# Queries and keys of an attention pair prepared three steps ahead of their scores instead of two

## The chip, the cores and the metric

The kernel runs on one core of a Trainium2 chip. A core has a matmul engine (PE), three engines for elementwise work (DVE, ACT, POOL) and a queue engine (SP) that issues transfers; each takes its own instructions in order, and they wait for each other on semaphores. The metric is device time in microseconds; lower is better.

## The reference

The input is a batch of 4 images of 32 x 32 tokens with 128 channels. The first layer is a shifted-window transformer block; the second is a self-attention over all 1024 tokens of an image. The change touches the window attention of the first layer alone. Cut to that:

```python
xn = _layer_norm(x, norm1_g, norm1_b)
xs = jnp.roll(xn, (-4, -4), axis=(1, 2))
xw = xs.reshape(B, nH, 8, nW, 8, 128).transpose(0, 1, 3, 2, 4, 5).reshape(64, 64, 128)
qkv = xw @ qkv_w.T + qkv_b                     # 16 heads of 8 channels
q = _rope2d(q); k = _rope2d(k)                 # rotation by the place in the window
attn = jnp.einsum('bhnd,bhmd->bhnm', q * scale, k) + attn_mask
attn = softmax(attn, axis=-1)
out = jnp.einsum('bhnm,bhmd->bhnd', attn, v)
```

Then come the output projection, a residual, a second layer norm, a gated MLP, and the second layer.

## The kernel before, in words

Two windows of 64 tokens make a pair of 128 rows; there are 32 pairs. The first half of the program, up to about 190 us, works them off in steps. All five engines run the same `body(n, it, w)`, each with its own part, from step `FIRST` on; steps 0 to 11 and the last ones are written out, steps 12 to 27 are two turns of a loop of eight. Several pairs are in flight. In step n, with the lines of the profile:

- PE projects queries and keys of pair n+2 (L899, L901), turns the rows of pair n+1 (L937, four matmuls for queries and four for keys), computes the scores of pair n (mask through L909, products L918), the transposed scores of pair n-1 (L909, L930), the values of pair n-3 (L991), the value projection of pair n-1 (L899, L901), and turns the query rows of pair n once more, now with the maxima in them (L937).
- DVE rotates pair n+2 (`ta`, `tb`, L1082), copies the turned rows of pair n+1 to `qk_t` (L1094), takes the low part of the values (L1102), the row maxima of pair n (L1109) and their two halves (L1114, L1116), and normalises pair n-3 (L1127, L1131).
- POOL adds `rot` (L1287), then takes the low part of the probabilities (`p_lo`, L1295), then the low parts of the query and key rows (L1299 to L1301).
- ACT makes the high parts of the rows (`q_rows`, `k_rows`, by the helper at L1151), the exponentials (L1221), the copy `q_t` of the second turning, the high values and `p_hi` (all L1151).
- SP waits for the copy `qk_t` and issues four transfers (L869) that spread the turned keys over `k_t`, in zeros. The scores of the pair wait for all four.

The four transfers of pair n+1 are issued in step n and their wait on PE is at the scores of step n+1:

```python
pe.wait_ge(kz_ready[u], it * 64 + 64)
wait(pe, mlo_done, n)
scores(qk_t[:, u, 0], k_t[:, r], w, parts).then_inc(s_done, 1)
```

The tiles `ta`, `tb`, `rot`, `k_rows` and `qk_t` have two buffers, `q_rows` and `k_t` four.

Beside the steps runs the first layer norm, in eight chunks of four pairs: statistics on DVE (L1026, L1030), the reciprocal root on POOL (L1264 to L1269), the normalisation on ACT (`xn`, L1165), the turning on PE (L878), and `xn_all` on ACT and DVE (L1151, L1045). Chunks 2 to 7 are turned in steps 1, 3, ... 11. In the negative steps POOL also clears half of `k_t` (L1305). In the last steps the first pieces of the MLP are interleaved (`mlp_early`).

## Time and profile before

| | us |
|---|---|
| median of 3 runs | 404.51 (403.96 to 408.64) |
| the profiled execution, its own time | 403.14 |
| its span in the trace | 401.3 |
| PE busy | 349.9 (87%) |
| DVE busy | 301.4 (75%) |
| ACT busy | 271.5 (68%) |
| POOL busy | 270.8 (67%) |

PE is the busiest engine of the whole span, but its busy time counts pipelined matmuls in full. The stages have to be read one by one: the ramp up to about 37 us, the steps with layer norm chunks up to about 88 us, the steps without them up to about 176 us, the last steps with the first MLP work up to about 195 us, and then the MLP and the second layer, in which the change has no instruction.

### The profile page before, as it was taken

The numbers are of one execution on the slowest core, as the hardware profiler recorded it, in microseconds if no ns is written. First come the engines' busy times: TensorE is split into PE (matmuls) and PEld (weight loads), VectorE is DVE, ScalarE is ACT, GpSimd is POOL, SyncE is SP. The second block draws the span as 40 slices with busy tenths as digits, with TensorE's granted clock in tenths as the row PEclk, the third lists the DMA queues.
The fourth block names the chain that finished last, engine by engine and source line by source line (L and its number), as shares of the span: only waits on it lengthen the run. The fifth ranks groups of instructions, "written<-read, shape, count | busy, mean of one in ns | idle before, by whom it ended". The sixth has DMA issues, their size and how long they took to land.

```text
span 401.3 us, 12541 instructions
## 1 busy us (share of the span) xinstructions
PE 349.9 (87%) x4900; PEld 228.5 (57%) x4900; DVE 301.4 (75%) x830; ACT 271.5 (68%) x435; POOL 270.8 (67%) x322
## 2 busy tenths in 40 slices
PE   2668999998989999998779899999988989989592
PEld 0335666555555666666456456654565757667371
DVE  6758988888878888888757678787668797883424
ACT  2466888887868788886835644445478877868480
POOL 7477976666767777798586786755267775867340
PEclk9999999999999999999999999999999999999797
DMA  6701111001111000010000000000000011010102
GB/s 187 244 19 28 29 28 26 23 24 31 28 29 30 26 26 26 26 33 11 2 3 2 15 13 2 2 2 2 9 19 22 7 54 28 2 54 2 52 2 57
DMA packets 15597, 12.29 MB, mean 31 GB/s; under 512 B 3992, under 2 KB 14137, under 8 KB 15545
## 3 DMA queue, kind: packets, MB, share of 16 engines
q1 hardware_dynamic: 14208, 11.03, 9.5%
q8 instruction: 36, 0.59, 0.7%
q10 hardware_dynamic: 1336, 0.54, 0.5%
q14 instruction: 17, 0.13, 0.1%
HBM read 4.22 MB, written 2.10 MB: 16 GB/s over the span
## 4 chain that ended last, share of the span: by engine, by line
PE 63%; DVE 16%; ACT 7%; issue 5%; DMA 4%; POOL 3%; SPq 1%; DVEq 0%; ACTq 0%; POOLq 0%
PE ps L359 8%; PE ps L1577 7%; PE ps L909 6%; PE ps L937 5%; PE ps L991 5%; PE ps L930 4%; PE ps L918 3%; PE ps L899 3%; DMA k_t<-qk_t 3%; PE ps L377 3%; PE ps L901 2%; DVE ob L1701 2%; DVE mx L1670 2%; PE ps L1417 2%; PE ps L373 2%
## 5 line engine op out<-in xcount | busy, mean ns | idle before, releaser
L1752 POOL TENSOR_TENSOR el<-e,eh 128x1024 f16<-128x1024 f32 x28 | 59.6, 2130 | 31.7 <-ACT eh L1744 31.4
L1295 POOL TENSOR_TENSOR p_lo<-e_buf,p_hi 128x1024 f16<-128x1024 f32 x32 | 68.2, 2130 | 4.8 <-ACT p_hi L1151 2.8
L359 PE MATMUL ps<-y_t,fc_w 128*128 128x512 f16 x192 | 46.2, 380 | 5.2 <-POOL al L273 2.5
L1287 POOL TENSOR_TENSOR rot<-ta,tb 128x256 f32<-128x256 f32 x32 | 23.3, 728 | 39.6 <-DVE tb L1082 38.8
L1109 DVE TENSOR_REDUCE ps<-ps 128x16 f32<-128x1024 f32 x32 | 39.4, 1232 | 8.3 <-PE ps L918 7.5
L1735 ACT ACTIVATE e<-ps 128x1024 f32<-128x1024 f32 x32 | 32.6, 1020 | 19.1 <-PE ps L1566 18.7
L1577 PE MATMUL ps<-val,eh 128*128 128x129 f16 x512 | 38.4, 225 | 7.8 <-DVE ob L1701 7.2
L909 PE MATMUL ps<-mask,identb 128*128 128x512 bf16 x128 | 39.4, 390 | 6.6 <-DMA k_t<-qk_t 6.5
L1221 ACT ACTIVATE e_buf<-ps 128x1024 f32<-128x1024 f32 x32 | 32.7, 1023 | 15.3 <-PE ps L930 15.1
L1577 PEld LDWEIGHTS ps<-val,eh 128*128 128x128 f16 x512 | 32.3, 100 | 18.6 <-issue 11.0
L288 POOL TENSOR_TENSOR hl<-hid,hh 128x512 f16<-128x512 f32 x24 | 27.7, 1158 | 20.4 <-DVE yn L566 11.2
L677 ACT ACTIVATE sg<-ps,fc_bias 128x512 f32<-128x512 f32 x32 | 21.9, 685 | 23.2 <-PE ps L359 23.0
L1670 DVE TENSOR_REDUCE mx<-ps 128x1 f32<-128x1024 f32 x24 | 29.3, 1223 | 8.8 <-PE ps L1550 8.4
L1151 ACT ACTIVATE p_hi<-e_buf 128x1024 f16<-128x1024 f32 x32 | 33.8, 1057 | 0.8
L1744 ACT ACTIVATE eh<-e 128x1024 f16<-128x1024 f32 x32 | 33.7, 1054 | 0.7
L359 PEld LDWEIGHTS ps<-y_t,fc_w 128*128 128x128 f16 x192 | 17.0, 98 | 27.9 <-issue 6.1
L937 PE MATMUL ps<-ident,q_rows 128*128 128x128 f16 x256 | 26.3, 227 | 6.5 <-DVE q_rows L1116 3.6
L529 DVE SCALAR_TENSOR_TENSOR hid<-ps,fc_bias,sg 128x512 f32<-128x512 f32 x32 | 23.8, 746 | 10.2 <-ACT sg L677 5.4
L899 PE MATMUL ps<-qkv_w,xn_all 128*128 128x128 f16 (+1 forms) x192 | 27.7, 254 | 2.5 <-DVE xn_all L1045 1.8
L930 PEld LDWEIGHTS ps<-q_t,k_t 128*64 128x64 f16 x1024 | 18.7, 112 | 13.6 <-issue 13.6
L1151 ACT ACTIVATE q_t<-ps 128x512 f16<-128x512 f16 x32 | 19.1, 596 | 10.4 <-PE ps L937 10.1
L1577 PE MATMUL ps<-val,el 128*128 128x129 f16 x256 | 23.8, 226 | 0.0
(164 smaller groups left out, 985.0 us busy)
## 6 DMA issues: line engine op xcount, KB each, us to landing
k_t<-qk_t SPq DMA_DIRECT2D x126, 32.0 KB, 1.9
x_all<-in_x SPq DMA_DIRECT2D x8, 256.0 KB, 4.4
out<-ob SPq DMA_DIRECT2D x8, 192.0 KB, 2.1
yr<-xr SPq DMA_DIRECT2D x16, 64.0 KB, 2.0
mask_f<-in_mask SPq DMA_DIRECT2D x1, 512.0 KB, 3.5
fc_w<-in_fc_w SPq DMA_DIRECT2D x1, 512.0 KB, 5.5
out<-ob SPq DMA_DIRECT2D x4, 128.0 KB, 1.9
fc_w<-in_fc_w SPq DMA_DIRECT2D x1, 256.0 KB, 5.4
```

The source lines that it names most:

```text
L359: last = pe.matmul(ps[:, bank, :], fc1_w16[:, ws, 128 * block_:128 * block_ + 128], y_t[:, v, ys, :], start=(n == 0), stop=(n == 2))
L899: pe.matmul(out, xn_all[:, at(i, 1), xs, :].rearrange("p a q -> p (a q)"), qkv_w16[:, ws, cols], start=(n == 0), stop=False, skip_group_ch ...
L909: pe.matmul(ps[:, bank + b, :].rearrange("p (h k) -> p h k", h=8), identb[:], mm, start=(part == 0), stop=False, skip_group_check=True)
L930: last = pe.matmul(ps[rows, ST_BANK + h // 8, WTOK * (h % 8):WTOK * (h % 8) + WTOK], keys[:, h % 4, h // 4, rows], queries[:, h // 4, rows ...
L937: last = pe.transpose(out[:, c, :], rows[:, 4 * c:4 * c + 4, :].rearrange("p h r -> p (h r)"), ident16[:])
L1109: dve.tensor_reduce(mx_ps, ps[:, S_BANK:S_BANK + 2, :].rearrange("p b (h k) -> p (b h) k", h=8), AX.X, ALU.max).then_inc(max_done, 1)
L1151: return act.activation(out, in_, ACT.Copy)
L1295: pool.tensor_tensor(p_lo[:, u], e_buf[:, u], p_hi[:, u], ALU.subtract).then_inc(plo_done, 1)
L1577: return pe.matmul(pv4[:, j, i, 0:DIM + 1], weights[:, T % H_BUFS, 128 * n:128 * n + 128], val[:, b % 2, part, m, 0:DIM + 1], start=first, ...
L1670: dve.tensor_reduce(mx[:, k:k + 1], two(S4), AX.X, ALU.max, negate=True).then_inc(max4_done, 1)
L1744: act.activation(eh[:, T % H_BUFS, :], e4[:, T % E_BUFS, :], ACT.Copy).then_inc(eh_done, 1)
L1752: pool.tensor_tensor(el[:, T % H_BUFS, :], e4[:, T % E_BUFS, :], eh[:, T % H_BUFS, :], ALU.subtract).then_inc(el_done, 1)
```

## The change

The preparation of queries and keys moves up by one pair. In step n PE now projects pair n+3 and turns the rows of pair n+2, DVE rotates n+3 and copies n+2, POOL and ACT make the rows of n+3, and SP issues the transfers of pair n+2. The first step is -3. `qk_t` gets four buffers, and the semaphore of the transfers is one per buffer of `k_t`. In step 0 this part stands behind the work on the pair's own scores instead of ahead of it. The chunk statistics that were pinned to steps -2 and -1 stay behind the same pieces of work, so their step numbers change.

The core of the diff (PE, DVE and ACT wrap the moved piece in a local function, called at the head of a step, and in step 0 further down):

```diff
-        kz_ready = [sem(f"kz_ready{u}") for u in range(2)]
+        kz_ready = [sem(f"kz_ready{k}") for k in range(BUFS)]
...
-            qk_t = tmp("qk_t", [128, 2, 2, 4, 128], F16)
+            qk_t = tmp("qk_t", [128, BUFS, 2, 4, 128], F16)
...
-            FIRST, LAST = -2, PAIRS + 2
+            FIRST, LAST = -3, PAIRS + 2
...
-                        for j in range(2 if at_step(n, -1) else 4):
+                        for j in range(2 if at_step(n, -2) else 4):
                             rows = slice(ROWS * j, ROWS * j + ROWS)
-                            sp.dma_start(k_t[rows, (r + 1) % BUFS, j], qk_t[rows, (r + 1) % 2, 1]).then_inc(kz_ready[(r + 1) % 2], 16)
+                            sp.dma_start(k_t[rows, k, j], qk_t[rows, k, 1]).then_inc(kz_ready[k], 16)
...
+                        if valid(n, -3):
+                            wait(pe, rope_done, n + 3)
+
+                            pe.wait_ge(ln_ready, (n + 3) // TPC + 1 if isinstance(n, int) and n < LOOP_FROM else CHUNKS)
+                            project(qkv_ps[:, 0:2 * DIM], n + 3, slice(0, 2 * DIM)).then_inc(qk_done, 1)
...
+                        if valid(n, -2):
+                            wait(pe, lo_done, n + 3)
+                            wait(pe, qt_ready, n + 2)
+                            if ln_chunk(n, 1):
+                                pe.wait_ge(ln_ready, ln_chunk(n, 1) + 1)
+                            turn(t1_ps[:, 0], q_rows[:, (r + 2) % BUFS])
+                            turn(t1_ps[:, 1], k_rows[:, u]).then_inc(t1_done, 1)
+
+                    if not at_step(n, 0):
+                        rows_turned()
                     if valid(n, 0):
 
                         if at_step(n, 0):
                             pe.wait_ge(mask_lo if parts > 1 else mask_hi, 1)
-                        pe.wait_ge(kz_ready[u], it * 64 + 64)
+                        pe.wait_ge(kz_ready[r], it * 64 + 64)
                         wait(pe, mlo_done, n)
-                        scores(qk_t[:, u, 0], k_t[:, r], w, parts).then_inc(s_done, 1)
+                        scores(qk_t[:, r, 0], k_t[:, r], w, parts).then_inc(s_done, 1)
...
+                    if at_step(n, 0):
+                        rows_turned()
                     if valid(n, 0):
                         wait(pe, mlo_done, n + 1)
                         wait(pe, q2_ready, n)
                         turn(t2_ps, q_rows[:, r]).then_inc(t2_done, 1)
...
-                    if valid(n, -2):
-
-                        pool.wait_ge(hi_done, n + 3)
-                        pool.tensor_tensor(q_rows[:, k, :, 16:24], rot[:, u, 0], q_rows[:, k, :, 0:8], ALU.subtract)
+                    if valid(n, -3):
+
+                        pool.wait_ge(hi_done, n + 4)
+                        pool.tensor_tensor(q_rows[:, k, :, 16:24], rot[:, v, 0], q_rows[:, k, :, 0:8], ALU.subtract)
...
+                    if at_step(n, -2):
+                        ln_rstd_of(2)
                     if at_step(n, -1):
-                        ln_rstd_of(2)
                         pool.memset(k_t[:, 2:BUFS].bitcast(F32), 0.0).then_inc(keys_set, 1)
                         ln_rstd_of(3)
```

How the ramp is reordered shows best in the instructions. On POOL, from the end of chunk 2's reciprocal root on, the kernel before has (the L1264 to L1269 rows are chunk 3, L1287 is `rot` of pair 2; the three instructions between the branches run only where the mask needs more parts):

```order
L1305 MEMSET k_t 128x2048
L1264 TENSOR_TENSOR veps<-mv,ln_const 128x4 [waits ln_stats]
L1265 TENSOR_TENSOR nmean<-mv,ln_const 128x4
L1267 TENSOR_TENSOR rstd<-veps,ln_const 128x4 [waits ln_pool]
L1269 TENSOR_TENSOR nmr<-nmean,rstd 128x4 [waits ln_pool]
L1309 TENSOR_LOAD mask_any [waits mask_known]
L1309 COMPARE_AND_BRANCH
L1311 TENSOR_TENSOR mrest<-mask_f,mask 128x1024 [waits mask_hi]
L1316 CAST mask<-mrest 128x1024 [waits mask_mid]
L1319 TENSOR_TENSOR mask<-mrest,mask 128x1024 [waits mask_mid]
L1309 UNCONDITIONAL_BRANCH
L1287 TENSOR_TENSOR rot<-ta,tb 128x256 [waits lo_done,rope_done]
```

and the changed kernel:

```order
L1311 TENSOR_TENSOR rot<-ta,tb 128x256 [waits lo_done,rope_done]
L1323 TENSOR_TENSOR q_rows<-rot,q_rows 128x16x8 [waits hi_done]
L1324 MEMSET q_rows 128x16x2
L1325 TENSOR_TENSOR k_rows<-rot,k_rows 128x16x8
L1330 MEMSET k_t 128x2048
L1287 TENSOR_TENSOR veps<-mv,ln_const 128x4 [waits ln_stats]
L1288 TENSOR_TENSOR nmean<-mv,ln_const 128x4
L1290 TENSOR_TENSOR rstd<-veps,ln_const 128x4 [waits ln_pool]
L1292 TENSOR_TENSOR nmr<-nmean,rstd 128x4 [waits ln_pool]
L1334 TENSOR_LOAD mask_any [waits mask_known]
L1334 COMPARE_AND_BRANCH
```

The whole work on pair 2, with its wait for ACT (`hi_done`), now stands ahead of the clearing of `k_t` and of chunk 3.

On PE, right behind the scores of pair 0 (L918), the kernel before has: the second turning of pair 0, the projection of pair 3, the turning of pair 2, the scores of pair 1.

```order
L937 MATMUL ps<-ident,q_rows 128x128 [waits mlo_done]
L937 MATMUL ps<-ident,q_rows 128x128 x3
L899 MATMUL ps<-qkv_w,xn_all 128x256 [waits ln_ready,rope_done]
L899 MATMUL ps<-qkv_w,xn_all 128x256 x2
L901 MATMUL ps<-qkv_b,sel 128x256
L937 MATMUL ps<-ident,q_rows 128x128 [waits qt_ready,lo_done]
L937 MATMUL ps<-ident,q_rows 128x128 x3
L937 MATMUL ps<-ident,k_rows 128x128 x4
L909 MATMUL ps<-mask,identb 128x512 [waits mlo_done,kz_ready1]
```

The changed kernel has projected pair 3 and turned pair 2 by then; from the second turning of pair 0 on:

```order
L938 MATMUL ps<-ident,q_rows 128x128 [waits mlo_done]
L938 MATMUL ps<-ident,q_rows 128x128 x3
L900 MATMUL ps<-qkv_w,xn_all 128x256 [waits ln_ready,rope_done]
L900 MATMUL ps<-qkv_w,xn_all 128x256 x2
L902 MATMUL ps<-qkv_b,sel 128x256
L938 MATMUL ps<-ident,q_rows 128x128 [waits qt_ready,lo_done]
L938 MATMUL ps<-ident,q_rows 128x128 x3
L938 MATMUL ps<-ident,k_rows 128x128 x4
L910 MATMUL ps<-mask,identb 128x512 [waits mlo_done,kz_ready1]
```

The rows read alike, but the projection is that of pair 4 and the turning that of pair 3: the scores of pair 1 now stand behind the finished rows of pair 3 (`lo_done`) instead of those of pair 2.

## Rows read from the trace of the kernel before

**Rows 1.** Waits of the first 210 us: who waited for whom, total us, times, longest

```profile
DVE ta L1082 <- PE ps L901: 10.2, 27, 1.2
...
PE ps L909 <- DMA k_t<-qk_t: 6.5, 7, 2.2
```

**Rows 2.** The line of SP's transfers: issue time and landing, min/median/max

```profile
L869 SPq DMA_DIRECT2D k_t<-qk_t x126: 507/592/1777, 18.0 to 181.1; - x126
...
DMA to landing us min/median/max: 1.8/1.9/3.7
```

**Rows 3.** Chain of waits, 124 to 132 us: start, us, what

```profile
124.89 0.61 DVE qk_t L1094
...
127.34 3.00 DMA k_t<-qk_t
```

**Rows 4.** Waits of PE alone, 90 to 170 us

```profile
PE ps L909 <- DMA k_t<-qk_t: 3.3, 4, 1.1
```

**Rows 5.** Timeline of PE, mask matmuls ahead of the scores: start, us, [idle before <-releaser]

```profile
72.02 0.60 PE L909 MATMUL ps<-mask,identb 128*128 128x512 bf16 x2 [0.49 <-DMA k_t<-qk_t]
...
94.33 0.61 PE L909 MATMUL ps<-mask,identb 128*128 128x512 bf16 x2 [1.06 <-DMA k_t<-qk_t]
...
135.08 0.59 PE L909 MATMUL ps<-mask,identb 128*128 128x512 bf16 x2
...
139.91 0.59 PE L909 MATMUL ps<-mask,identb 128*128 128x512 bf16 x2
...
168.45 0.60 PE L909 MATMUL ps<-mask,identb 128*128 128x512 bf16 x2
```

**Rows 6.** Timeline of DVE in a step without a stall

```profile
163.31 0.42 DVE L1082 TENSOR_TENSOR ta<-ps,rope 128x256 f32<-128x256 f32 x1 [0.29 <-PE ps L901]
...
163.99 0.68 DVE L1094 COPY qk_t<-ps 128x1024 f16<-128x1024 f16 x1
```

**Rows 7.** Timeline of all engines, 10 to 37 us, the ramp

```profile
20.07 1.80 POOL L1305 MEMSET k_t<- 128x2048 f32 x1
20.17 1.65 ACT L1165 ACTIVATE xn<-x_all,nmr,rstd 128x128 f32<-128x128 f32 x4 [2.67 <-POOL nmr L1269]
...
21.83 0.20 POOL L1264 TENSOR_TENSOR veps<-mv,ln_const 128x4 f32<-128x4 f32 x1
...
23.35 0.20 POOL L1269 TENSOR_TENSOR nmr<-nmean,rstd 128x4 f32<-128x4 f32 x1
...
24.12 0.72 POOL L1287 TENSOR_TENSOR rot<-ta,tb 128x256 f32<-128x256 f32 x1 [0.58 <-issue]
24.88 0.42 ACT L1151 ACTIVATE q_rows<-rot 128x256 f16<-128x256 f32 x1 [3.06 <-POOL rot L1287]
...
25.51 1.63 ACT L1165 ACTIVATE xn<-x_all,nmr,rstd 128x128 f32<-128x128 f32 x4
...
26.12 0.42 POOL L1301 TENSOR_TENSOR k_rows<-rot,k_rows 128x128 f16<-128x128 f32 x1
...
27.06 0.61 PE L937 MATMUL ps<-ident,q_rows 128*128 128x128 f16 x4
...
27.59 0.58 ACT L1151 ACTIVATE q_t<-ps 128x512 f16<-128x512 f16 x1
...
27.89 1.06 PE L909 MATMUL ps<-mask,identb 128*128 128x512 bf16 x2
...
29.99 1.23 DVE L1109 TENSOR_REDUCE ps<-ps 128x16 f32<-128x1024 f32 x1 [0.94 <-PE ps L918]
...
33.28 0.40 PE L937 MATMUL ps<-ident,q_rows 128*128 128x128 f16 x4
...
33.74 0.59 PE L909 MATMUL ps<-mask,identb 128*128 128x512 bf16 x2
```

**Rows 8.** Busy time, granted clock (third from the right) and DMA of a stretch of the ramp

```profile
26.00:31.00 5.00, 5.00 (x29) 2.89 (x28) 3.99 (x18) 3.90 (x9) 3.75 (x12) 1.00 0.06 17
```

**Rows 9.** Timeline of DVE, the last copy of turned rows

```profile
178.16 0.69 DVE L1094 COPY qk_t<-ps 128x1024 f16<-128x1024 f16 x1
```

More of the change, by code:

```diff
@@ L944, in body @@
                     v = 1 - u
-                    if valid(n, -2):
-                        wait(pe, rope_done, n + 2)
-                        pe.wait_ge(ln_ready, (n + 2) // TPC + 1 if isinstance(n, int) and n < LOOP_FROM else CHUNKS)
-                        project(qkv_ps[:, 0:2 * DIM], n + 2, slice(0, 2 * DIM)).then_inc(qk_done, 1)
-                    if at_step(n, -2):
-                        pe.wait_ge(mask_top, 1)
-                        pe.matmul(ps[0:1, T1_BANK, 0:1], mask_max[:], ln_const[:, 2, 0:1], start=True,
-                                  stop=True).then_inc(mask_summed, 1)
@@ L1075, in body @@
                     v = 1 - u
-                    if valid(n, -2):
-                        dve.wait_ge(qk_done, n + 3)
-                        wait(dve, r_done, n + 1)
-                        x = qkv_ps[:, 0:2 * DIM].rearrange("p (a h d) -> p a h d", a=2, h=HEADS)
-                        for dst, k in ((ta, 0), (tb, 1)):
-                            last = dve.tensor_tensor(dst[:, u], x,
-                                                     rope[:, k].unsqueeze(2).broadcast_to([128, 2, HEADS, HD]), ALU.mult)
-                        last.then_inc(rope_done, 1)
@@ L1097, in body @@
+                    if not at_step(n, 0):
+                        rows_rotated()
                     if valid(n, 2):
@@ L1190, in body, with rows_high @@
                         mlp_act(act)[2](LAST - n)
-                    if valid(n, -2):
-                        act.wait_ge(r_done, n + 3)
-                        copy(q_rows[:, (r + 2) % BUFS, :, 0:16].rearrange("p h (r d) -> p h r d", r=2),
-                             rot[:, u, 0].unsqueeze(2).broadcast_to([128, HEADS, 2, HD]))
-                        wait(act, t1_done, n + 1)
-                        copy(k_rows[:, u].rearrange("p h (r d) -> p h r d", d=HD)[:, :, 0:3:2, :],
-                             rot[:, u, 1].unsqueeze(2).broadcast_to([128, HEADS, 2, HD])).then_inc(hi_done, 1)
+                    def rows_high():
+                        if valid(n, -3):
+                            act.wait_ge(r_done, n + 4)
+                            copy(q_rows[:, (r + 3) % BUFS, :, 0:16].rearrange("p h (r d) -> p h r d", r=2),
+                                 rot[:, v, 0].unsqueeze(2).broadcast_to([128, HEADS, 2, HD]))
+                            wait(act, t1_done, n + 2)
+                            copy(k_rows[:, v].rearrange("p h (r d) -> p h r d", d=HD)[:, :, 0:3:2, :],
+                                 rot[:, v, 1].unsqueeze(2).broadcast_to([128, HEADS, 2, HD])).then_inc(hi_done, 1)
+                    if not at_step(n, 0):
+                        rows_high()
+                    if at_step(n, -3):
+                        ln_hi_of(1)
                     if at_step(n, -2):
-                        ln_hi_of(1)
-                    if at_step(n, -1):
                         act.wait_ge(qt_ready, 1)
@@ L1226, in body @@
                         copy(q_t2[:, u], t2_ps).then_inc(q2_ready, 1)
+                    if at_step(n, 0):
+                        rows_high()
                     if valid(n, 1):
@@ L1281, in body @@
                     u = r % 2
-                    k = (r + 2) % BUFS
-                    if valid(n, -2):
-                        pool.wait_ge(rope_done, n + 3)
-                        wait(pool, lo_done, n + 2)
+                    v = 1 - u
+                    k = (r + 3) % BUFS
+                    if valid(n, -3):
+                        pool.wait_ge(rope_done, n + 4)
+                        wait(pool, lo_done, n + 3)
                         pool.tensor_tensor(
-                            rot[:, u].rearrange("p a h (s d) -> p (a h) s d", s=2),
-                            ta[:, u].rearrange("p a h (s d) -> p (a h) s d", s=2),
-                            tb[:, u].rearrange("p a h (s d) -> p (a h) s d", s=2)[:, :, ::-1, :], ALU.add)\
+                            rot[:, v].rearrange("p a h (s d) -> p (a h) s d", s=2),
+                            ta[:, v].rearrange("p a h (s d) -> p (a h) s d", s=2),
+                            tb[:, v].rearrange("p a h (s d) -> p (a h) s d", s=2)[:, :, ::-1, :], ALU.add)\
                             .then_inc(r_done, 1)
```

74 lines of the change are left out of this document (42 added, 32 removed).

## The prediction

> **What bounds the kernel now.** I read the page's table of engines first, then the waits, then the chain of waits, then the timelines of single steps. The change touches only the window attention, up to about 190 us, so I looked there for what ends last.
>
> The list of waits has one entry that the change is aimed at: PE idle ahead of the mask matmuls of the scores, 6.5 us in seven times, released by SP's transfers of `k_t`; the longest is 2.2 us [rows 1]. The longest one is in the ramp, at the very first scores, where nothing is ahead of it to hide it. Four of the seven, 3.3 us together, lie between 90 and 170 us [rows 4]. Of the other two, 0.49 us is at 72 us [rows 5] and about 0.5 us in the last steps (6.5 less 2.2, 3.3 and 0.49).
>
> Why these waits exist is in the transfer's own numbers. SP needs 592 ns to issue one transfer, the four of a pair are issued one behind the other, and one takes 1.9 us from issue to landing in the median, 3.7 us at worst [rows 2]. So from the end of the copy `qk_t` to the fourth landing it is about three issues with their gaps, 1.85 us (from 125.50, the end of the copy, to 127.34 [rows 3]), and 1.9 us: 3.75 us. A step lasts 4.76 us: from 139.91 to 168.45 there are six [rows 5]. The copy of the next pair's rows stands early in the step and its scores early in the next, so 3.75 us just fits. The stall comes when a landing is late: at 127.34 it took 3.00 us, to 130.34 [rows 3], and PE stood.
>
> A step without a stall is held by another loop. DVE takes the maxima, PE turns the queries with them and projects the next pair, and DVE waits for this projection, 0.29 us, before it rotates [rows 6]; over all it is 27 waits and 10.2 us [rows 1]. The rest of the step DVE works without a gap. In steady state the change moves each piece by exactly one pair, and the order on PE and DVE within a step stays. So I expect 4.76 us of a quiet step to stay as it is.
>
> **The change part by part.**
>
> *The stalls of the middle.* With a step more between issue and use, a landing has 3.75 + 4.76 us, and the worst latency seen, 3.7 us, is covered. All four stalls, 3.3 us [rows 4], go. A check from the steps: from 94.33 to 135.08 there are eight, 40.75 us [rows 5], against 8 x 4.757 = 38.05: 2.7 us over, to which the 1.06 us ahead of 94.33 [rows 5] has to be added, 3.76 us in all; a part of that is at the loop's edge and stays. The maxima on DVE, which the stalled scores hold up, stand behind DVE's own work and would come a little later than PE could serve them. So I take 3.2 us, between 2.5 and 3.8.
>
> *The other three.* The first one, 2.2 us, stays: pair 0's transfers are issued as early as before. The one at 72 us is worth nothing: in that odd step PE next waits for ACT's normalised chunk anyway, and in the chain of waits the stretch from 37 to 88 us runs over ACT. The one in the last steps lies beside DVE's first MLP work: nothing.
>
> *The ramp.* Here I expect a loss. Step 1 now holds the scores of pair 1 behind the turning of pair 3, which needs pair 3's finished rows, and these stand behind more work than it seems. I follow it with the durations of [rows 7].
> - POOL now adds `rot` of pair 2 (0.72) where the clearing of `k_t` was, at 20.07: done at 20.8. Its low parts wait for ACT, which is in the normalisation of chunk 2 from 20.17 for 1.65: until 21.8. From ACT's high part to the end of POOL's low part it was 24.88 to 26.54, 1.66: low parts done at 23.5.
> - Then the clearing, 1.80: 25.3. Then chunk 3's reciprocal root, 21.83 to 23.55, 1.72: 27.0, where it was 23.55.
> - ACT waits for that with chunk 3. Before, this began at 25.51 and the copy `q_t` at 27.59, 2.08 later; now 27.0 and 29.1. Behind `q_t` (its successor can follow 0.5 us later) come the high parts of pair 3, 29.6, and POOL's low parts end 1.66 later: 31.3.
> - PE turns pair 3 at 31.3, where it turned pair 2 at 27.06, and the maxima of pair 1 began 2.93 us behind that turning (29.99). So they now begin at 34.3, 4.3 us later, if the matmuls run as slowly as they did there. They may not: the mask's two took 1.06 us at 27.89 and 0.59 at 33.74, a turning and the step to the mask 0.83 at 27.06 and 0.46 at 33.28. At the quick pace the 2.93 us become about 1.7 (0.46, and 1.2 for mask, scores and start of the maxima, from 1.06 + 1.04 at the slow one), and the loss is 3.0 us.
>
> The bounds are thus 3.0 and 4.3 us; a wait of DVE for chunk 2's high half, which ACT makes after pair 4's rows, may add some tenths. I take 3.6 us. What follows, steps 2 to 11, keeps its order, so nothing there takes up the delay.
>
> The granted clock is shown as 1.00, the upper level of 2.4 GHz, from 26 to 31 us, with PE busy all 5 us [rows 8]; the durations above say that the lower level of 1.2 GHz fits these matmuls better, and that it rose near 31 us, after five busy microseconds. The changed kernel is busy from 21.7 to about 27 and then stands for some 4 us. The Trainium skill (TensorE: Matmul & The Clock Gate, "HAM oscillation — how this bites in real kernels") says that waits between short stretches of matmuls throw the clock back to half, each time. By it the loss would be the full 4.3 us and the next step slow as well; that is a rival below.
>
> *The last steps.* What is prepared a pair earlier is missing at the end. Step 29 has no projection and no rotation: the 0.29 us of waiting and the two rotations, 163.31 to 163.99, 0.68 us [rows 6]; step 30 has no turning and no copy, 0.69 us [rows 9], of which PE's turning next to it gives about as much. DVE is the one that ends last there, and two short PE pieces go with it. I take 1.4 us back, between 0.7 (POOL and ACT, full with the first MLP work, become late instead) and 1.7.
>
> *At nothing:* four buffers for `qk_t`, four semaphores (the same number of transfers and of waits), the moved issue on SP (its queue is empty between two groups of four), `q_rows` with four buffers that now holds one pair more: its overwriting stands behind the projection, and that behind the last turning on PE.
>
> **The sum.** +3.6 - 3.2 - 1.4 = -1.0 us. The profiled execution took 403.14 us, so 402.1 us against its own time. The median of the runs shown is 404.51, 1.4 us above it; with that I predict 403.5 us, which is no change that can be told (the measurement tells about 2%, 8 us).
>
> **The rivals.**
>
> *A, the loss in the ramp does not come* (13%). The stalls and the last steps give 4.6 us, and chunk 3, POOL and ACT have slack that I have not seen. For it: ACT waited 3.06 us at 24.88 [rows 7]. Against it: that very wait is the one that is filled up. Time 399.9 us.
>
> *B, slower: PE stays at the lower clock level through steps 1 and 2* (12%). The place is the standing of PE between the projection of pair 4 and the turning of pair 3. It decides if the standing undoes or postpones the rise seen near 31 us. Then the loss at the first maxima is 4.3 us, and the step behind it, 4.76 us with PE nearly full at the quick pace, gets longer: 80% (1.06 for 0.59 us [rows 7]) over two thirds of it, since the last third may be quick again, is 2.5 us. 4.3 + 2.5 - 3.2 - 1.4 = +2.2: 406.7 us. For it: the same matmuls were slow until 31 us in spite of much work; against it: they ran without a gap for 5 us in the changed kernel too, before the standing.
>
> *C, slower: the stalls are not cured by an earlier transfer* (18%). They sit in steps near the loop's two turns, and something else, such as an engine that resumes late there, could take their place. The price is that the 3.2 us are not won: +3.6 - 1.4 = +2.2, 406.7 us; at half of it 405.1 us. It decides from about 1 us of replaced stalls on. For it: 2.7 us of excess against 2.2 us of stalls in those eight steps. Against it: the chain names the landing itself [rows 3]. The Trainium skill (DMA: Bandwidth & Descriptors, "Anatomy of one DMA — SWDGE (gpsimd) path") gives a transfer a fixed cost of about 2.0 us that scales with nothing. The median landing agrees; the 3.00 and 3.7 us do not, and by the page there would be no late landing to hide and the time would be this rival's.
>
> **Chances and range.** My forecast, the sum with its bounds: 57%. Its bounds make 403.5 - 1.4 and + 1.6 us: with 3.0 for the ramp and 3.8 and 1.7 won it is 402.0, with 4.3, 2.5 and 0.7 it is 405.6. A reaches down to 399.9, B and C up to 406.7. Runs of one kernel differ by 0.5 us beside the outlier. A range of 400.0 to 407.0 leaves out less than 2 in 10. A change by over 2% needs 8 us, more than all stalls or twice the loss in the ramp: faster 2%, slower 2%, within 2% 96%.
>
> **What the changed profile would show.** The wait of PE's mask matmuls for the transfers is one entry of 2.2 us or a little more, in the ramp; steps from 90 us on are 4.76 us each, and 0.3 us more at the loop's edge. The maxima of pair 1 begin at 33 to 34.5 us instead of 29.99, with PE idle for about 4 us ahead of the turning of pair 3, released by POOL; chunk 3's reciprocal root ends near 27. The last maxima, against those of pair 28, come 1.4 us sooner. The forecast is wrong if the maxima of pair 1 are under 2 us late, if stalls of more than 1 us in sum remain after 90 us, or if the quiet step is not 4.76 us.

## The result, and the profile after

The changed kernel takes **408.17 us** in the median of 20 runs (404.01 to 411.68); the kernel before, in 20 runs on the same chip, 405.36 us (401.29 to 408.64). The ratio is 1.0078, with a 95% interval of 1.0054 to 1.0101: slower by 3.2 us by the ratio, 2.8 us by the medians, and 4.7 us above the 403.5 us predicted, outside the range of 400.0 to 407.0. Ratios, here and below, leave out the slow executions, those over 1.5% above the quickest of their kernel (one of these 20 of the changed kernel, seven of e1's 12, four of e7's 12, at most one of 12 elsewhere; 27 of 99 of the kernel before beside them), and medians leave out none. The profiled execution took 408.22 us, its span 406.4 us, where before stood 403.14 and 401.3.

Up to the last maxima on DVE things went much as forecast. Behind them, where the change has no instruction, the rest is lost. First the ramp, in the changed kernel's timeline, to be laid beside [rows 7]:

```profile
19.84 0.72 POOL L1311 TENSOR_TENSOR rot<-ta,tb 128x256 f32<-128x256 f32 x1
...
22.70 0.43 POOL L1325 TENSOR_TENSOR k_rows<-rot,k_rows 128x128 f16<-128x128 f32 x1
23.06 1.80 POOL L1330 MEMSET k_t<- 128x2048 f32 x1
...
26.36 0.20 POOL L1292 TENSOR_TENSOR nmr<-nmean,rstd 128x4 f32<-128x4 f32 x1
26.59 1.65 ACT L1181 ACTIVATE xn<-x_all,nmr,rstd 128x128 f32<-128x128 f32 x4 [4.41 <-POOL nmr L1292]
...
30.87 0.60 PE L938 MATMUL ps<-ident,q_rows 128*128 128x128 f16 x4 [4.24 <-POOL k_rows L1325]
...
31.70 1.06 PE L910 MATMUL ps<-mask,identb 128*128 128x512 bf16 x2
...
33.80 1.23 DVE L1123 TENSOR_REDUCE ps<-ps 128x16 f32<-128x1024 f32 x1 [1.16 <-PE ps L919]
```

The maxima of pair 1 begin at 33.80 us instead of 29.99, and the mask's matmuls again take 1.06 us. The maxima of pair 0 began 0.25 us sooner than before (23.50 against 23.75), so the ramp's loss is 4.06 us. The profile records the clock at its lower level from 28.75 to 35.57 us.

The waits of PE on DMA, first 210 us, to be laid beside [rows 1]: one is left of seven, that of the ramp.

```profile
PE ps L910 <- DMA k_t<-qk_t: 2.2, 1, 2.2
```

The last steps, DVE's maxima of pairs 28, 30 and 31 and the one new wait on PE:

```profile
170.31 1.23 DVE L1123 TENSOR_REDUCE ps<-ps 128x16 f32<-128x1024 f32 x1
...
173.03 0.40 PE L938 MATMUL ps<-ident,q_rows 128*128 128x128 f16 x4 [0.52 <-POOL k_rows L1325]
...
179.27 1.23 DVE L1123 TENSOR_REDUCE ps<-ps 128x16 f32<-128x1024 f32 x1
184.74 1.23 DVE L1123 TENSOR_REDUCE ps<-ps 128x16 f32<-128x1024 f32 x1
```

Before, these three stood at 169.99, 179.51 and 185.03. So at pair 28 the changed kernel was 0.32 us behind, at the last maxima 0.29 us ahead.

One of the vanished waits for `k_t` stood in step 31. PE's mask matmuls of pair 31, before and after:

```profile
182.98 0.61 PE L909 MATMUL ps<-mask,identb 128*128 128x512 bf16 x2 [0.52 <-DMA k_t<-qk_t]
```

```profile
182.01 0.59 PE L910 MATMUL ps<-mask,identb 128*128 128x512 bf16 x2
```

Then comes the loss. The tail of the kernel before, from 186 us (PE: last turning, the small fc1-bias product L517, scores, the projection behind them, first fc1; DVE: scaling of the bias; POOL: low parts of the probabilities):

```profile
186.84 0.40 PE L937 MATMUL ps<-ident,q_rows 128*128 128x128 f16 x4 [0.49 <-DVE q_rows L1116]
189.48 0.17 DVE L668 TENSOR_SCALAR fc_bias<-fc_bias 128x4 f32<-128x4 f32 x1
189.52 2.13 POOL L1295 TENSOR_TENSOR p_lo<-e_buf,p_hi 128x1024 f16<-128x1024 f32 x1 [1.12 <-ACT p_hi L1151]
190.60 0.33 PE L899 MATMUL ps<-qkv_w,xn_all 128*128 128x128 f16 x3
194.36 1.46 PE L359 MATMUL ps<-y_t,fc_w 128*128 128x512 f16 x6 [1.47 <-DVE y_t L579]
```

The same of the changed kernel:

```profile
186.55 0.40 PE L938 MATMUL ps<-ident,q_rows 128*128 128x128 f16 x4 [1.19 <-DVE q_rows L1130]
186.78 1.90 PE L517 MATMUL ps<-g1b,fc_w 128*128 128x1 f32 x16
189.06 1.01 PE L931 MATMUL ps<-q_t,k_t 128*64 128x64 f16 x32
189.23 2.25 POOL L1319 TENSOR_TENSOR p_lo<-e_buf,p_hi 128x1024 f16<-128x1024 f32 x1 [0.59 <-ACT p_hi L1167]
189.73 1.78 DVE L668 TENSOR_SCALAR fc_bias<-fc_bias 128x4 f32<-128x4 f32 x1
192.07 0.50 PE L900 MATMUL ps<-qkv_w,xn_all 128*128 128x128 f16 x3 [1.16 <-DVE v_lo L1116]
196.40 2.72 PE L359 MATMUL ps<-y_t,fc_w 128*128 128x512 f16 x6 [0.85 <-DVE y_t L579]
```

Two things differ. DVE's scaling of four columns took 0.17 us where it started 0.04 us ahead of POOL's low parts, and takes 1.78 us where it starts 0.50 us behind them; it ends at 191.51, POOL at 191.48. And PE's matmuls turn slow: the first fc1 takes 2.72 us for 1.46. The windows of the changed kernel show the clock at its lower level (length, busy time and count of PE, its weight load, DVE, ACT, POOL; then the granted clock, DMA share, GB/s):

```profile
187.00:192.00 5.00, 3.91 (x74) 3.31 (x73) 4.89 (x9) 3.14 (x5) 3.89 (x2) 0.72 0.00 0
192.00:197.00 5.00, 4.08 (x66) 3.21 (x67) 2.24 (x8) 3.75 (x7) 2.42 (x2) 0.50 0.01 3
197.00:202.00 5.00, 5.00 (x49) 2.75 (x48) 3.42 (x9) 2.96 (x6) 1.85 (x2) 0.76 0.00 0
```

The same windows before, all at 1.00:

```profile
187.00:192.00 5.00, 5.00 (x117) 4.33 (x116) 3.86 (x13) 3.99 (x8) 3.53 (x2) 1.00 0.01 3
192.00:197.00 5.00, 3.06 (x57) 1.97 (x55) 3.10 (x9) 4.92 (x8) 4.12 (x3) 1.00 0.00 0
197.00:202.00 5.00, 3.43 (x24) 1.76 (x24) 4.41 (x15) 2.63 (x5) 1.71 (x6) 1.00 0.00 0
```

From the last maxima to the first fc1 it was 9.33 us (185.03 to 194.36) and is 11.66 (184.74 to 196.40), 2.3 us more; from there to the end of the span it was 206.9 and is 210.0 us, 3.1 us more. -0.3 + 2.3 + 3.1 is the difference of the spans, 5.1 us. In the changed kernel the clock is at its lower level from 189.17 to 199.41 us and again from 206.24 to 209.65, where the third fc1 takes 2.74 us for 1.47; before it is nowhere so between 30.9 us, where the records begin, and 230 us.

### The profile page after: what moved, and what is told of

The parts are those of the page before. It is cut to its first block, busy times and chain, and to the rows that moved or that the text cites. A ratio compares the mean times of both kernels' runs of the same rounds, so it can differ in the third digit from the quotient of the medians.

```text
span 406.4 us, 12549 instructions
## 1 busy us (share of the span) xinstructions
PE 354.0 (87%) x4900; PEld 230.9 (57%) x4900; DVE 303.2 (75%) x830; ACT 271.5 (67%) x435; POOL 270.9 (67%) x322
## 4 chain that ended last, share of the span: by engine, by line
PE 61%; DVE 16%; POOL 8%; ACT 7%; issue 5%; DMA 1%; DVEq 0%; POOLq 0%; ACTq 0%
PE ps L359 9%; PE ps L1602 7%; PE ps L910 5%; PE ps L938 5%; PE ps L997 4%; PE ps L931 4%; PE ps L900 3%; PE ps L919 3%; PE ps L377 3%; DVE ob L1726 2%; PE ps L902 2%; DVE mx L1695 2%; PE ps L1442 2%; PE ps L373 2%; ACT xn L1181 2%
## 5 line engine op out<-in xcount | busy, mean ns | idle before, releaser
L359 PE MATMUL ps<-y_t,fc_w 128*128 128x512 f16 x192 | 48.7, 395 | 5.4 <-POOL al L273 3.3
L900 PE MATMUL ps<-qkv_w,xn_all 128*128 128x256 f16 (+1 forms) x192 | 27.9, 256 | 3.5 <-DVE xn_all L1053 1.8
L938 PEld LDWEIGHTS ps<-ident,q_rows 128*128 128x128 f16 x256 | 14.9, 99 | 18.8 <-POOL k_rows L1325 9.5
```

What stands on the lines that cost most here:

```text
L359: last = pe.matmul(ps[:, bank, :], fc1_w16[:, ws, 128 * block_:128 * block_ + 128], y_t[:, v, ys, :], start=(n == 0), stop=(n == 2))
L900: pe.matmul(out, xn_all[:, at(i, 1), xs, :].rearrange("p a q -> p (a q)"), qkv_w16[:, ws, cols], start=(n == 0), stop=False, skip_group_ch ...
L938: last = pe.transpose(out[:, c, :], rows[:, 4 * c:4 * c + 4, :].rearrange("p h r -> p (h r)"), ident16[:])
```

## The experiments

The theories were: **R**, the ramp loses because pair 1's scores stand behind pair 3's rows, and these behind chunk 3's root on POOL; **T**, the clock falls near 189 us because PE has less to do in the last steps or stands there; **P**, it falls because the four-column scaling meets POOL; and, formed after the first eight kernels, **D**: there are two places, and either alone can make it fall. One is PE standing ahead of the last turning, the other PE standing while DVE is held up by POOL. Each kernel was timed in 12 runs (e8 in 6, which gave no ratio), in three groups (e1 to e4, e5 to e8, e9 to e12), each on a chip of its own beside the kernel before: 406.1, 406.2 and 405.3 us in the median. The changed kernel itself was not timed again with them, so across groups the ratios are what can be compared. Semaphore increments are left out of the cuts of e5 and e10. The table has the median, the ratio to before with its interval, and from the profile: how long PE stood ahead of the last turning, how long the scaling took, the time from the last maxima to the first fc1, and the mean granted clock in a window of 10 us from about 3 us behind the last maxima.

| kernel | median us | ratio (95%) | stood | scaling | to fc1 | clock |
|---|---|---|---|---|---|---|
| before | 405.36 | 1 | 0.49 | 0.17 | 9.33 | 1.00 |
| after | 408.17 | 1.0078 (1.0054-1.0101) | 1.19 | 1.78 | 11.66 | 0.56 |
| e1 | 410.63 | 1.0024 (0.9975-1.0073) | 1.19 | 1.35 | 11.52 | 0.67 |
| e2 | 409.14 | 1.0051 (1.0009-1.0092) | 0 | 1.78 | 11.66 | 0.66 |
| e3 | 402.75 | 0.9927 (0.9891-0.9964) | 0 | 0.17 | 9.99 | 1.00 |
| e4 | 406.15 | 1.0014 (0.9979-1.0049) | 1.19 | 1.79 | 11.66 | 0.52 |
| e5 | 406.92 | 1.0045 (0.9993-1.0097) | 1.20 | 0.16 | 9.98 | 0.83 |
| e6 | 403.19 | 0.9970 (0.9911-1.0030) | 0 | 0.16 | 9.56 | 1.00 |
| e7 | 407.02 | 1.0042 (0.9990-1.0095) | 0.85 | 0.16 | 11.53 | 0.66 |
| e8 | 409.89 | none | 1.19 | 1.78 | 11.66 | 0.66 |
| e9 | 403.82 | 0.9993 (0.9959-1.0027) | 0 | 0.16 | 9.57 | 1.00 |
| e10 | 406.79 | 1.0044 (1.0010-1.0079) | 0.70 | 2.00 | 11.53 | 0.65 |
| e11 | 403.39 | 0.9947 (0.9915-0.9979) | 0 | 0.16 | 9.93 | 1.00 |
| e12 | 401.90 | 0.9933 (0.9893-0.9973) | 0 | 0.16 | 9.55 | 1.00 |

### e1, the last pair's projection and turning put back into steps 29 and 30

```diff
+ if at_step(n, PAIRS - 3):
+     pe.wait_ge(rope_done, PAIRS)
+     project(qkv_ps[:, 0:2 * DIM], PAIRS - 1, slice(0, 2 * DIM))
+ if at_step(n, PAIRS - 2):
+     pe.wait_ge(qt_ready, PAIRS)
+     turn(t1_ps[:, 0], q_rows[:, (r + 1) % BUFS])
+     turn(t1_ps[:, 1], k_rows[:, v])
```

> The changed kernel with PE's work of steps 29 and 30 put back: a projection and a turning of pair 31 are done a second time there, with results that nobody uses. Theory T (the time behind 190 us is lost because PE's clock falls to its lower level at about 189 us, and it falls because PE has less to do in the last steps): no fall at 189 us in most runs, the first piece of the MLP as fast as before, and the time 3 to 5 us below the changed kernel, about 404. Rival P (the fall is a matter of where the program stands in time, or comes from the ramp): the fall stays and the time is that of the changed kernel or up to 0.6 us more, 408 to 409.

The clock still falls, and PE still stands 1.19 us ahead of the last turning. The work put back is not what kept the clock up; T falls as far as it speaks of the work. It also shows that the missing projection and turning are not why PE stands: with both back it stands just as long.

### e2 and e3, unused matmuls ahead of the last turning, in the changed kernel and in the one before

```diff
+ if at_step(n, PAIRS - 1):
+     for _ in range(20):
+         pe.matmul(ps[:, T2_BANK, 384:512], ident16[:], ident16[:], start=True, stop=True,
+                   skip_group_check=True)
```

> The changed kernel with 20 matmuls of 128 columns that nobody uses in step 31, where PE waits 1.2 us for the maxima ahead of the last turning. Theory T (the clock falls because PE stands or does little there): the granted clock stays at the upper level from 189 to 199 us in most runs, time 3 to 5 us below the changed kernel, about 404. Rival P (not PE's idleness there): fall and time stay, 408. Rival M (the time behind 190 us is lost to something else than the clock): the clock stays up but the time stays 408.

> The kernel before with the same 20 unused matmuls in step 31. The profiled run of before had no fall of the clock at 189 us, but its runs spread from 401.3 to 408.6 us. Theory T: a part of the runs of before has the fall as well, and the filling takes it out: spread under 3 us and the time 1 to 3 us below before, about 403. Rival P: no difference from before, the same spread.

The same fill did nothing for the changed kernel and took 0.7% off the kernel before. In e2 the matmuls run at full pace through the scores, and then PE stands for DVE:

```profile
189.33 0.69 PE L931 MATMUL ps<-q_t,k_t 128*64 128x64 f16 x32
...
192.33 0.50 PE L900 MATMUL ps<-qkv_w,xn_all 128*128 128x128 f16 x3 [1.61 <-DVE v_lo L1120]
```

The projection that took 0.33 us takes 0.50 again. In this profile the clock falls at 191.17 us, 0.4 us into that standing. So the standing filled is not the only cause. The kernel before seems to have falls there too, in part of its executions, since e3 gains (e7 below shows one such execution); its times still spread over 5.2 us, where under 3 was expected. The fill is a little too long for the kernel before: it pushes the last turning from 1.81 to 2.47 us behind the last maxima, and the first fc1 from 9.33 to 9.99 us behind them.

### e4, pair 1's scores ahead of pair 3's rows

In step 1 PE, DVE and ACT now do the moved piece at the place where step 0 has it, behind the scores (shown for PE; two of its waits in step 1 are moved with it; POOL's order stays as in the changed kernel).

```diff
- if not at_step(n, 0):
+ if not at_step(n, 0) and not at_step(n, 1):
...
- if at_step(n, 0):
+ if at_step(n, 0) or at_step(n, 1):
```

> The changed kernel with the moved piece of step 1 behind that step's own scores, as the change already does for step 0 (on PE, DVE and ACT). Theory R (the ramp's loss of 4.1 us is the scores of pair 1 standing behind the finished rows of pair 3): PE's wait of 4.2 us ahead of that turning no longer holds up the maxima of pair 1, they begin below 31 us, the clock does not fall in the ramp, and the time is 2 to 4 us below the changed kernel. Rival (the loss is the order on POOL and comes back one step later): the maxima of pair 1 are early, those of pair 2 begin at 40 us as in the changed kernel, no gain in time.

Its maxima of pairs 1, 2 and 31:

```profile
29.03 1.20 DVE L1125 TENSOR_REDUCE ps<-ps 128x16 f32<-128x1024 f32 x1
...
37.81 1.23 DVE L1125 TENSOR_REDUCE ps<-ps 128x16 f32<-128x1024 f32 x1
...
182.92 1.23 DVE L1125 TENSOR_REDUCE ps<-ps 128x16 f32<-128x1024 f32 x1
```

Pair 1 is 4.8 us sooner than after the change; pair 2, at 37.81 against 40.29, keeps 2.5 of it, and with the start 0.28 us later, the last maxima are 1.8 us sooner. R holds: the order in step 1 made the larger part of the loss. By the ratios (1.0014 for 1.0078, the difference uncertain by 0.42%) it is worth 0.64%, 2.6 us. The tail is as bad as ever.

### e5, the bias scaled from PSUM

```diff
- dve.tensor_tensor(fc1_bias[:], ps[:, at_bank(0), 0:2 * HBLK], fc1_b[:], ALU.add)
+ dve.tensor_tensor(fc1_bias[:, HBLK:], ps[:, at_bank(0), HBLK:2 * HBLK], fc1_b[:, HBLK:], ALU.add)
+ dve.tensor_tensor(ps[:, at_bank(0), 0:HBLK], ps[:, at_bank(0), 0:HBLK], fc1_b[:, 0:HBLK], ALU.add)
...
- dve.tensor_scalar(fc1_bias[:, 0:HBLK], fc1_bias[:, 0:HBLK], WSCALE, None, ALU.mult)
+ dve.tensor_scalar(fc1_bias[:, 0:HBLK], ps[:, at_bank(0), 0:HBLK], WSCALE, None, ALU.mult)
```

> The changed kernel, with one alteration ahead of the first MLP stage: the scaling of the four-column fc1 bias on DVE reads its operand from PSUM, where the sum is now left, and writes to SBUF as before; the result is the same. Theory P (the last stage starts late because this small instruction meets POOL's p_lo and stands for 1.78 us, where it took 0.17 us in the kernel before): with an operand in PSUM it no longer waits for POOL, takes about 0.2 us, the first fc1 matmuls start about 1.5 us sooner, and if the fall of the clock at 189 us hangs on that standing, it goes too: 403 to 405 us, 4 us less than the changed kernel's 408.2. Rival T (the fall of the clock comes from the thin PE work of the last two attention steps and has nothing to do with this instruction): the instruction gets short, the clock still falls near 189 us, and the time stays within 1.6 us of the changed kernel's. Rival W (the wait only moves): DVE's next instruction with operands in SBUF stands in its place, and nothing is gained.

```profile
186.64 0.40 PE L939 MATMUL ps<-ident,q_rows 128*128 128x128 f16 x4 [1.20 <-DVE q_rows L1131]
189.16 0.85 PE L932 MATMUL ps<-q_t,k_t 128*64 128x64 f16 x32
189.89 0.16 DVE L669 TENSOR_SCALAR fc_bias<-ps 128x4 f32<-128x4 f32 x1
194.81 1.46 PE L359 MATMUL ps<-y_t,fc_w 128*128 128x512 f16 x6 [0.98 <-DVE y_t L579]
```

0.16 us instead of 1.78, although POOL's low parts began at 189.31: it is the operand in SBUF that made the scaling wait. The Trainium skill (SBUF — State Buffer, "🔬 SBUF: two separate sides") says that GpSimd and VectorE, the latter in a two-port mode or with two SBUF inputs, share one pair of ports as an exclusive lock for a whole instruction. The ends at 191.51 (scaling) and 191.48 (POOL) in the changed kernel agree, and so does the release by PSUM. So does DVE's addition just ahead (L665), with one input in PSUM and one in SBUF: it took 0.17 us at 189.53 in the changed kernel, with POOL at work since 189.23. The first fc1 begins 1.6 us sooner than after the change. But the scores, 0.85 us, show the clock falling (at 189.50 us), without any standing behind them: P does not explain the fall. The time is 406.92 us, where P expected 403 to 405.

### e6, e4, e2 and e5 together

> The changed kernel with three alterations at once: scores of pair 1 ahead of the rows of pair 3 in step 1 (as in e4), 20 unused 128-column matmuls ahead of the last turning (as in e2), and the fc1 bias scaled from PSUM (as in e5). If the three losses are separate (ramp 2.5 us regained, bias 1.6 us, falls near 189 and 206 us some 2 us): 402 to 403 us, below the kernel before (406.1 in the last comparison). If the falls of the clock stay whatever stands there: about 405 us, no difference from the kernel before.

403.19 us, by the ratios 1.08% or 4.4 us below the changed kernel. In the tail the clock now stays up until 202 us. By time the three edits do no more than add up (0.64% for e4, 0.27% for e2, 0.33% for e5, 1.24% in sum); it was the clock in the profile, which neither e2 nor e5 alone had kept up, that gave D.

### e7, the bias from PSUM in the kernel before

Edit as in e5.

> The kernel before, with the fc1 bias scaled from PSUM and nothing else altered. There the instruction took 0.17 us in the profiled execution, since POOL's p_lo started 40 ns after it. If other executions lose that race (runs of the kernel before lie between 401 and 410 us with the clock between 0.989 and 0.965), their slow tail should go: a median 1 to 3 us below the kernel before, 403 to 405 us. If the spread has another cause, the times stay as they are, within 1 us of 406.1.

No gain (0.9990 to 1.0095): there is no sign that the kernel before often loses that race. Its profile is the useful part, since it shows a fall in the kernel before itself, in an execution where PE stood longer ahead of the last turning:

```profile
186.95 0.40 PE L938 MATMUL ps<-ident,q_rows 128*128 128x128 f16 x4 [0.85 <-DVE q_rows L1117]
187.18 2.81 PE L517 MATMUL ps<-g1b,fc_w 128*128 128x1 f32 x16
```

With 0.49 us of standing the sixteen small matmuls took 1.90 us, with 0.85 us 2.81. The length of the standing alone does not set this: behind 1.19 us in the changed kernel they took 1.90 us and the clock fell only 2.6 us behind the start of the last turning, where here it fell 1.0 us behind it.

The profiles of the unfilled kernels before also tell where the standing comes from. PE's wait for `k_t` in step 31 and its standing ahead of the last turning add up to 0.52 + 0.49 = 1.01 us in the kernel before, 0.17 + 0.85 = 1.02 us here, and 0.32 + 0.70 = 1.02 us in e10. Without the wait it stands for all of it: 1.19 us after the change.

### e8, unused matmuls in the ramp

```diff
+ if at_step(n, 1):
+     pe.wait_ge(mlo_done, 1)
+     for _ in range(14):
+         pe.matmul(..., identb[:], mask16[:, 0, 0, 0:1, :].broadcast_to([128, 8, WTOK]), start=True, stop=True, ...)
```

> The changed kernel, with 14 unused 512-column matmuls in step 1, in the time in which PE stands ahead of the turning of pair 3; their result is overwritten by the mask. Theory R (the standing comes from POOL's low parts, and makes the clock fall from 28.5 to 35.4 us): the maxima of pair 1 stay at 33 to 34 us, since POOL sets them, but the clock doesn't fall there, the turning, the mask and the scores behind it go at the upper level, and pair 2's maxima come 0.5 to 1.5 us sooner than 40.29: 0.5 to 1.5 us in all. Rival (the level costs nothing there, as DVE and ACT set the next steps): maxima of pair 2 at 40.3 within 0.2 us, no gain. In both cases the falls near 189 and 206 us stay.

```profile
30.96 0.40 PE L938 MATMUL ps<-ident,q_rows 128*128 128x128 f16 x4 [0.23 <-POOL k_rows L1331]
...
31.42 0.59 PE L910 MATMUL ps<-mask,identb 128*128 128x512 bf16 x2
...
32.62 1.23 DVE L1129 TENSOR_REDUCE ps<-ps 128x16 f32<-128x1024 f32 x1 [0.30 <-PE ps L919]
39.38 1.23 DVE L1129 TENSOR_REDUCE ps<-ps 128x16 f32<-128x1024 f32 x1
```

The turning is released at the same time by POOL, but mask 0.59 us instead of 1.06, and the maxima of pairs 1 and 2 come 1.2 and 0.9 us sooner. So 1.2 of the 4 us were the clock, which had fallen while PE stood (28.75 us; in e8 it stays up there). My expectation for pair 1 (no change) was wrong. The total, in six runs between 402.6 and 413.1, tells nothing.

### e9 and e11, fill and bias together, in the changed kernel and in the one before

> The changed kernel with both alterations at its tail, the 20 unused 128-column matmuls ahead of the last turning (as in e2) and the fc1 bias scaled from PSUM (as in e5), and none in the ramp. Theory D (two places, each of which alone makes the clock fall between 187 and 202 us: PE standing 1.19 us ahead of the last turning, and PE standing behind the last-but-one scores while DVE is held up by POOL's p_lo): each alteration alone gained about 1 us or nothing, since the other place was left; both together keep the clock up until 200 us, the first fc1 matmuls begin at 194.5 to 195.5 us (196.40 in the changed kernel) and take 1.46 us, and the median is 404 to 405.5 us, 3 to 4 us below the changed kernel's 408.2. Rival E (the two only add up): 1 to 1.5 us below, 406.7 to 407.2 us. Theory R: the maxima of pair 1 stay at 33.8 us.

> The kernel before with the same two alterations at its tail as in e9, and nothing of the change. e3, with the fill alone, stood at 402.75 us. If the race is lost in some executions even with the fill, the median falls by another 0.5 to 1 us, to about 402 us, and the slow end of its runs (404 to 406 us) goes. If it is never lost there: 402.5 to 403 us. Either way it should be below e9, by the 4 us of the ramp less the 3.5 us of the stalls less 0.6 us of the last steps, which is nearly nothing: within 1 us of e9 if e9 is as theory D has it, 2 us or more below it if not.

e9's tail:

```profile
184.72 1.23 DVE L1128 TENSOR_REDUCE ps<-ps 128x16 f32<-128x1024 f32 x1
...
189.79 0.16 DVE L669 TENSOR_SCALAR fc_bias<-ps 128x4 f32<-128x4 f32 x1
190.51 0.34 PE L901 MATMUL ps<-qkv_w,xn_all 128*128 128x128 f16 x3
194.29 1.45 PE L359 MATMUL ps<-y_t,fc_w 128*128 128x512 f16 x6 [1.48 <-DVE y_t L579]
```

The last maxima stand where they stood after the change, at 184.72, and the span ends at 399.6 instead of 406.4. In ratios, e2 and e5 alone took 0.27% and 0.33% off the changed kernel, both together 0.85% (1.0078 to 0.9993, the difference uncertain by 0.41%), 3.4 us. That the tail costs the changed kernel time is clear of the noise. That the two places are more than a sum is not: 0.27 + 0.33 would give 1.0018, inside e9's interval. The profile agrees with D, with no fall of the clock between 35 and 376 us, but it is the quickest of e9's executions: its mean granted clock is 0.992, the median over the twelve 0.974 (0.985 in e11), so in most of them the clock still falls somewhere. In the kernel before the same two edits took 0.53%. So by the ratios the tail costs the changed kernel 0.3% (1.3 us) more than it costs the kernel before, and that difference is uncertain by 0.5%: the timed runs do not show it by themselves. What is left between e9 and e11 is 0.4 us by the medians and 0.46% (1.9 us) by the ratios, with each ratio uncertain by 0.35%. In e11 the fill delays the last turning, as in e3, so this is rather too little than too much.

### e10, the race lost in the kernel before

```diff
- dve.tensor_tensor(fc1_bias[:], ps[:, at_bank(0), 0:2 * HBLK], fc1_b[:], ALU.add)
+ for c in range(0, 2 * HBLK, 2):
+     last = dve.tensor_tensor(fc1_bias[:, c:c + 2], ps[:, at_bank(0), c:c + 2], fc1_b[:, c:c + 2], ALU.add)
```

> The kernel before, with one alteration: the fc1 bias is added in four instructions of two columns in place of one of eight, with the same result, which only delays the scaling behind it by 0.2 us. In the profiled execution of before the scaling began 0.04 us ahead of POOL's p_lo and took 0.17 us. Theory P (the loss behind 185 us is this race, lost): it now begins behind p_lo, takes 1.6 to 1.9 us, PE stands over 1 us behind its last-but-one scores, the clock falls near 190 us, and the kernel before gets 2 to 4 us slower: 408 to 410 us with 406.1 for before. Rival (the block is hidden behind other work): the scaling takes as long, the first fc1 matmuls begin within 0.4 us of 194.36, and the median stays within 1 us.

```profile
187.77 2.13 POOL L1297 TENSOR_TENSOR p_lo<-e_buf,p_hi 128x1024 f16<-128x1024 f32 x1 [1.12 <-ACT p_hi L1153]
187.93 2.00 DVE L670 TENSOR_SCALAR fc_bias<-fc_bias 128x4 f32<-128x4 f32 x1
190.49 0.50 PE L901 MATMUL ps<-qkv_w,xn_all 128*128 128x128 f16 x3 [1.48 <-DVE v_lo L1104]
194.81 2.72 PE L359 MATMUL ps<-y_t,fc_w 128*128 128x512 f16 x6 [0.85 <-DVE y_t L579]
```

A delay of 0.16 us behind POOL's start, and the kernel before shows a tail much like the changed kernel's: the scaling 2.00 us, a wait of 1.48, the first fc1 2.72, and 11.53 us from the last maxima to fc1. The clock falls at 189.00 us, just as PE comes to a stand behind its values, not in the course of that standing. PE had also stood 0.70 us ahead of the last turning in this execution, against 0.49 in that of the kernel before, so the profile does not tell which of the two brought the fall. It is slower by 0.44% (0.10 to 0.79), 1.5 us by the medians, less than the 2 to 4 I expected.

### e12, e9 with POOL's old order

```diff
+ if at_step(n, -1):
+     pool.memset(k_t[:, 2:BUFS].bitcast(F32), 0.0).then_inc(keys_set, 1)
+     ln_rstd_of(3)
```

(the same two lines are taken out behind the rows of pair 2)

> e9 with one more alteration: POOL clears k_t and makes chunk 3's reciprocal root ahead of the rows of pair 2, as it did before the change, and not behind them. Theory R (the 4 us of the ramp come from chunk 3's root, which stands behind POOL's new low parts, and through it from ACT's late rows of pair 3): the root ends near 23.6 us instead of 26.56, PE turns pair 3 at about 29.3 us instead of 30.87, and the maxima of pair 1 begin at 32 to 32.5 us instead of 33.80; the gain of 1.5 us is kept to the end, so 1 to 1.5 us below e9. Rival (the rows of pair 2, now later on POOL, take it back): the maxima of pair 1 at 33.5 us or later, no gain.

```profile
22.11 1.01 POOL L1295 TENSOR_TENSOR rstd<-veps,ln_const 128x4 f32<-128x4 f32 x1
...
29.55 0.61 PE L939 MATMUL ps<-ident,q_rows 128*128 128x128 f16 x4 [1.28 <-POOL k_rows L1333]
...
32.47 1.23 DVE L1128 TENSOR_REDUCE ps<-ps 128x16 f32<-128x1024 f32 x1 [1.17 <-PE ps L920]
```

The root of chunk 3 (its middle instruction at 22.11 us) ends at 23.40 us instead of 26.56, the turning of pair 3 at 29.55 instead of 30.87, the maxima of pair 1 at 32.47 instead of 33.80, and the last ones 1.3 us sooner too. 401.90 us is 1.9 us below e9, the lowest median of all, 0.67% below the kernel before (0.27 to 1.07) and, by the ratios, 1.45% or 5.9 us below the changed kernel. But most of the 0.67% is the two edits of the tail, which take 0.53% off the kernel before as well (e11). That the earlier preparation, with the ramp in this order, gains anything over e11 is not shown: 0.14%, with each ratio uncertain by 0.3 to 0.4%.

## Why the prediction was wrong

- **The stalls of the middle**, 3.2 us predicted: all went, and from pair 1 to pair 28 the changed kernel wins 3.49 us on the one before (136.51 against 140.00 us). From 90 us on it is 3.4 us, and the quiet steps stay at 4.75 to 4.80 us. Right; rival C is out.
- **The ramp**, 3.6 us predicted, 4.06 measured, with POOL, ACT and PE waiting as written: root done at 26.56 (27.0 predicted), turning of pair 3 at 30.87 (31.3), maxima at 33.80 (34.3). I took a value between the quick and the slow pace of the matmuls; they ran at the slow pace, since the clock fell while PE stood, and e8 puts 1.2 us on it. That is the first part of rival B's mechanism. Its second part, 2.5 us for a longer step behind, did not come (pair 1 to 2 takes 6.49 us in both), though the clock was low until 35.57 us. By the section of the Trainium skill that the prediction names for it (TensorE: Matmul & The Clock Gate, "HAM oscillation — how this bites in real kernels") the loss would be the full 4.3 us. The trace agrees with the fall, and 4.3 is nearer to the 4.06 than my 3.6; that the next step would be slow as well the trace does not bear out.
- **The last steps**, 1.4 us predicted, 0.6 measured. Step 29 gave nothing: the turning of pair 31 waited 0.52 us for POOL's `k_rows` at 173.03. POOL being late was the reason given for the lower end, 0.7.
- **The sum at the last maxima** is thus -0.3 us where -1.0 was predicted.
- **The step that failed** has two sides. I summed up to the last maxima and put all behind them at nothing, since the change has no instruction there; it costs 5.4 us in the profiled executions. And I put the vanished wait for `k_t` in the last steps at nothing, because it lies beside DVE's work. The 0.52 us do not vanish, they move: PE gets to the last turning when DVE is still at the maxima and stands 1.19 us instead of 0.49. Beside it a race is lost. POOL starts its low parts 0.29 us sooner, as the last maxima do. DVE's scaling starts 0.25 us later, since DVE's `yn` (L566) ran 2.22 us for 1.69: it ends 0.85 us behind POOL's previous low parts in both kernels, and these end 0.24 us later. The race had been won by 0.04 us.
- **How far this is shown.** That the scaling waits for POOL with its input in SBUF, and costs 1.6 us to the first fc1, e5 shows. That the tail as a whole takes 0.85% from the changed kernel, e9 shows. That the clock falls because of these two standings is argued. In the six profiles with 0.85 us or more ahead of the last turning (after, e1, e4, e5, e7, e8) it had fallen before PE stood for DVE behind its values, if it stood there at all; the second place rests on e2 alone, since in e10 the clock fell as PE came to a stand. That the tail costs more than in the kernel before, only the profiles show.
- **The base**: 404.51 us was the median of three runs; over 20 it was 405.36, and that is 0.85 us of the 4.7. The 20 runs spread over 7 us, so 408.64 was no outlier and "0.5 us" too narrow. The sum at the last maxima is another 0.7 us, which leaves 3.1 us for what is behind them. The profiles say 5.4 because the one of before is a quick execution, 2.2 us below its median, and the one after an ordinary one. The recorded "- 1.4 and + 1.6" around 403.5 does not match its own ends, 402.0 and 405.6, which are 1.5 below and 2.1 above; no reading hangs on it.

Not settled: the medians say that the change costs 0.4 us where both tails are mended, the ratios 0.46%; I have no place for the difference. Nor did I try to raise the clock in the falls near 205 us, which some of the mended kernels keep: e6's profile has the third fc1 at 2.74 us instead of 1.47.

## What to carry to other kernels

A prediction's sum must go on to the end of the kernel: a piece that the edit does not touch still shifts against its neighbours, and one should look there for races won by a few hundredths of a microsecond and for engines that stand briefly. A wait that is cured ahead of a slow partner becomes a longer standing in front of it; here this went with a fall of the clock in the profiles. Where DVE and POOL run side by side on a critical path, look at the small DVE instructions: one of four columns, read from PSUM instead of SBUF, began the first fc1 1.6 us sooner. And an edit of the tail that helps should be tried on the kernel before too, or its gain is credited to the change.

## What the runs showed of the hardware

- A DVE instruction on four columns, 0.17 us of work, took 1.35 to 2.00 us with its input in SBUF when it began behind a long POOL instruction with SBUF operands (1.78 in the changed kernel, e2 and e8, 1.79 in e4, 1.35 in e1, 2.00 in e10), and 0.16 us with its input in PSUM (e5, e6, e7, e9 and e12, all with POOL at work).
- In the profiles of the changed kernel, e1, e4, e5, e7 and e8, PE stood 0.85 to 1.20 us ahead of the last turning, and the granted clock fell to half (1.2 of 2.4 GHz) 0.9 to 2.9 us behind the start of that turning. In e10 (0.70 us) it fell 3.9 us behind it, in e2 (no standing there) 4.4 us. Behind 0.49 us or none it did not fall in the kernel before, e3, e9, e11 and e12, nor in e6 until 202 us, although PE stood another 1.47 us ahead of the first fc1 in the kernel before and 1.48 in e9. A group of six 512-column matmuls took 2.72 us at the lower level and 1.46 at the upper. How much the clock falls differs from run to run of one kernel: the median over the timed runs of the mean granted clock was 0.973 to 0.977 before in the three groups, 0.963 after and 0.986 in e12.
- The profile shows the clock of the ramp before as 1.00 [rows 8], though the mask's matmuls took 1.06 us there and 0.59 us a few microseconds later. Durations of a known shape tell the level better than that column in the first 31 us.
